# Two-part x1, later statistics, weight pieces on POOL and a lighter tail in a transformer layer

## The chip, the cores and the metric

One core of a Trainium2 chip. The core has five engines that run side by side, each with its own instruction stream served in order: PE (TensorE, matrix products), DVE (VectorE), ACT (ScalarE), POOL (GpSimd) and SP (SyncE, which here only issues transfers). They meet through semaphores. The metric is the device time of one execution in microseconds; lower is better.

## The reference

One post-norm transformer layer on 16 batch elements of 256 positions and 256 channels, in float32:

```
qkv = x @ Wqkv + bqkv                  # 16 query heads of 16, 4 key/value heads (shared)
prob = softmax(q k / 16);  a = (prob v) @ Wout + bout
x1 = layernorm(x + a)
gate, up = split(x1 @ tern(w_gate_up).T)        # 2 x 1024 channels
h = rms_norm(silu(gate) * up)
out = layernorm(x1 + h @ tern(w_proj).T)
```

`tern` makes a weight ternary: in bfloat16, by groups of 64, scale = mean(abs(w)), q = clip(round(w / scale), -1, 1), and w + (q * scale - w) with the rounding of each step.

## The kernel before

Float32 products are made of two passes: a tensor is split into a high part, rounded to a shorter format, and a low part, the rest, and both are multiplied with the same weights. x1 (transposed) and h are split this way.

The work is cut into slots. Batch element b has its steps at fixed offsets from slot 8b, so 8 slots after one element the next one does the same step, and up to six elements are in the pipeline at once. Every engine has a function `slot(n)` that goes through its own steps in a written order; a step runs if slot n minus its offset falls on an element (`once`) or on a chunk s = 0 to 7 of one (`chunk`). Slots 0 to 63 and 128 to the end are written out, slots 64 to 127 are a loop of 16-slot bodies. What an engine does in a slot, and in which order, is fixed by this code; semaphores only make it wait.

The steps of one element that matter here, with their offsets:

- Attention: raw scores for the row maxima from offset 9 (`max_scores` on PE, `take_maximum` on DVE, two per slot, called i = 0 and 1: "max0" and "max1"), exponentials from 15, products with v from 16.
- Offset 27: output projection on PE (PROJ_O); DVE adds the residual (O_ADD, L890), takes the statistics (`bn_stats` L893, `bn_aggr` L897); POOL makes the reciprocal root (RSTD1, L944 and L922).
- Offset 28: DVE scales r1 to x1 (LN1_APPLY, L881). Offset 29: PE transposes x1 (X1_T, L552) into a bank of `short_ps`, ACT copies the high part (X1_HIGH). Offset 30: DVE makes the low part (X1_LOW, L765).
- Offsets 31 to 38, one chunk per slot: gate and up products on PE (`gate_up`, L507), tanh on ACT, gated (L817) and h_f (L824) on DVE; one slot later ACT makes h_hi and the square, POOL h_lo (L928) and the running sum of squares (L933); two slots later `down` on PE (L521).
- Offset 40: sum of squares over partitions, mean, root. Offset 42: second residual and statistics on DVE, root on POOL (RSTD2). Offset 44: POOL scales to y_out (LN2_APPLY, L940), SP stores.

The three banks `short_ps` are shared by all short products by a table (BANK_TABLE); the transpose of x1 uses the bank that max0 of the same slot has used before it, and waits until that maximum is taken.

The order on POOL within a slot (L924): h_lo and sum of squares; LN2_APPLY; RSTD1; ADD_BOUT; Q_LOW; the weight piece; INV; RSTD2. On DVE (L811): max0; gated; h_f; X1_LOW; SHIFT_SPLIT[0]; LN2_STATS; max1; MEAN_SQ; PV_DIVIDE; V_COPY; LN1_APPLY; SHIFT_SPLIT[1]; weight piece; O_ADD with the statistics; K_LOW.

The ternary weights are made in 12 pieces in slots 1 to 27: ACT reads a piece in slot W_READ (L661), one slot later DVE makes sums, scale and three tensor operations on w_hat (`tern_weights`, L790) and POOL two more (L957 to L963); PE transposes the piece (`turn_weights`, L452) four slots after the read and ACT places it one slot after that. `keep_clock` (L560) adds small products on PE in slots 2 to 29.

Of the kernel before, what the change touches and what calls it, by code (L numbers as in the profile page):

```python
# [76 lines left out]
O_ADD = 27  # L77
RSTD1 = 27
X1_HIGH = 29
# [26 lines left out]
W_READ = (1, 2, 3, 5, 8, 10, 12, 14, 16, 18, 20, 22)  # L106
W_MAKE, W_TURN, W_PLACE = 1, 4, 5
W_LATER = 9
CLOCK_FROM, CLOCK_TO = 2, 30

LAST = SLOTS * B + STORE
LOOP_FROM, BODY = 64, 2 * SLOTS
LOOPS = (SLOTS * B - LOOP_FROM) // BODY
# [71 lines left out]


def previous_use(slot, position, uses):

    for back in range(slot.t + 1):
        earlier = Slot(slot.t - back, slot.it)
        for use in sorted(uses, key=lambda u: -u[1]):
            st = earlier.once(use[0])
            if st and (back or use[1] < position):
                return st, use
    return None


def postln_layer(nc, x, Wqkv, bqkv, Wout, bout, w_gate_up, w_proj, out):  # L200
    ctx = ExitStack()
    with ctx:
# [17 lines left out]
        w_sign = sb("w_sign", [P, 2, PG, Q_GROUP], BF16)  # L220
        w_hat = sb("w_hat", [P, 2, PG, Q_GROUP], BF16)
        w_sum = sb("w_sum", [P, PG])
        w_scale = sb("w_scale", [P, PG], BF16)
        w_half = sb("w_half", [P, PG], BF16)
# [132 lines left out]
        def piece(n, later):  # L357

            return W_READ.index(n.t - later) if n.it is None and n.t - later in W_READ else None

        block = ctx.enter_context(nc.Block())

# [79 lines left out]
        def _(pe):  # L442
# [9 lines left out]
            def turn_weights(c):  # L452

                pe.wait_ge(w_pool, 2 * (c + 1))
                if c >= 2:
                    pe.wait_ge(w_ev, c - 1)
                flat = w_hat[:, c % 2].rearrange("p g e -> p (g e)")
# [49 lines left out]
            def gate_up(n, st):  # L507
                wait(pe, x1T_lo, st.count(1, 1))
                if st.it is None and st.b == 0 and st.s == 0:
                    pe.wait_ge(w_ev, len(pieces))  # L510
                if alternate(n, st) and n.t - SLOTS < TWO_BANKS and st.s == 1:
                    wait(pe, exp_done, SLOTS * B)
                wait(pe, h_done, st.count(8, st.s - 1 if n.it is None and n.t > TWO_BANKS else st.s))
                for half in range(2):
                    c = half * F + st.s * P
                    last = products(gate_up_bank(n, st, half),
                                    [wguT[:, k, c:c + P] for k in range(DT) for _ in range(2)],
                                    [x1T[a][:, st.par, k, :] for k in range(DT) for a in range(2)])
                last.then_inc(ffn_made, 1)
# [40 lines left out]
            def keep_clock(n, count):  # L560

                if n.it is not None or not CLOCK_FROM <= n.t < CLOCK_TO:
                    return
                turned = sum(at + W_TURN < n.t for at in W_READ)
                if turned:
                    pe.wait_ge(w_ev, turned - 1)
                for _ in range(count):
                    pe.matmul(turn_banks[turned % 2][:, 0, 0:P], ident[:], ident[:], start=True, stop=True)

            def slot(n):  # L570
# [63 lines left out]
                if (c := piece(n, W_TURN)) is not None:  # L634
                    turn_weights(c)
# [17 lines left out]
        def _(act):  # L653
# [5 lines left out]
            def read_weights(c):  # L659

                raw = pieces[c][0]  # L661
                act.wait_ge(w_loaded[c], 16)
                if c >= 2:
                    act.wait_ge(w_pool, 2 * (c - 1))
# [12 lines left out]
            def slot(n):  # L677
# [71 lines left out]
                if (c := piece(n, W_PLACE)) is not None:  # L749
# [10 lines left out]
        def _(dve):  # L760
# [18 lines left out]
            def shift_rows(n, st, half):  # L779
# [8 lines left out]
                                         ).then_inc(shift_split, 1)  # L788

            def tern_weights(c):  # L790
# [4 lines left out]
                dve.tensor_scalar(w_scale[:], w_sum[:], 1.0 / Q_GROUP, 1e-8, ALU.mult, ALU.max).then_inc(w_red, 1)  # L795
                dve.wait_ge(w_red, 3 * c + 2)
                dve.tensor_scalar(w_half[:], w_scale[:], 0.5, None, ALU.mult).then_inc(w_red, 1)
                dve.wait_ge(w_red, 3 * c + 3)
                if c >= 2:
                    dve.wait_ge(w_tr, c - 1)  # L800
                half = w_half[:].unsqueeze(2).broadcast_to([P, PG, Q_GROUP])
                scale = w_scale[:].unsqueeze(2).broadcast_to([P, PG, Q_GROUP])

                hat = w_hat[:, c % 2]
                for i, (a, b, op) in enumerate(((w_abs[:, c % 2], half, ALU.is_gt), (hat, scale, ALU.mult),
                                                (hat, w_sign[:, c % 2], ALU.mult))):
                    if i:
                        dve.wait_ge(w_dve, 3 * c + i)
                    dve.tensor_tensor(hat, a, b, op).then_inc(w_dve, 1)  # L809

            def slot(n):  # L811
                if st := n.chunk(MAX0):
                    take_maximum(n, st, 0)
                if st := n.chunk(GATE0):

# [3 lines left out]
                if st := n.chunk(H0):  # L819
# [5 lines left out]
                                      ).then_inc(h_done, 1)  # L825
                if st := n.once(X1_LOW):
                    wait(dve, x1T_hi, st.count(1, 1))
                    low(x1T[1][:, st.par], both(n, "x1"), x1T[0][:, st.par]).then_inc(x1T_lo, 1)
                if st := n.once(SHIFT_SPLIT[0]):
                    shift_rows(n, st, 0)  # L830
                if st := n.once(LN2_STATS):

# [54 lines left out]
                if st := n.once(O_ADD):  # L887
                    wait(dve, o_made, st.count(1, 1))
                    wait(dve, bout_added, st.count(1, 1))
                    dve.tensor_tensor(r1[:], both(n, "o"), res[:, st.par], ALU.add).then_inc(r1_done, 1)  # L890
                    wait(dve, r1_done, st.count(1, 1))
                    for t in range(TT):
                        dve.bn_stats(st1[:, t, :], r1[:, t, :]).then_inc(bn1_done, 1)  # L893
                    wait(dve, bn1_done, st.count(TT, TT))
                    dve.sem_inc(waited, 1)
                    for t in range(TT):
                        dve.bn_aggr(mv1[:, t, :], st1[:, t, :]).then_inc(var1_done, 1)  # L897
                if st := n.once(K_LOW):
# [7 lines left out]
        def _(pool):  # L906
# [17 lines left out]
            def slot(n):  # L924
                if st := n.chunk(H_LOW0):
# [3 lines left out]
                                       h_p[0][:, st.s % 4, :].bitcast(F32), ALU.subtract).then_inc(h_lo, 1)  # L929
                    if st.s:  # L930
# [26 lines left out]
                if (c := piece(n, W_MAKE)) is not None:  # L957

                    pool.wait_ge(w_dve, 3 * (c + 1))
                    hat = w_hat[:, c % 2]  # L960
                    pool.tensor_tensor(hat, hat, w_bf[:, c % 2], ALU.subtract).then_inc(w_pool, 1)
                    pool.wait_ge(w_pool, 2 * c + 1)
                    pool.tensor_tensor(hat, hat, w_bf[:, c % 2], ALU.add).then_inc(w_pool, 1)  # L963
# [33 lines left out]
```

## Time and profile before

| | |
|---|---|
| median of 3 runs | 621.06 us (619.04 to 621.45) |
| profiled execution | 616.0 us |
| its span, first to last instruction | 614.1 us |
| mean granted TensorE clock | 0.971 of full speed |
| busy: PE, DVE, ACT, POOL | 554.9, 442.1, 369.9, 327.6 us |
| chain that ended last: PE, DVE, issue, POOL | 68%, 20%, 5%, 3% |

The profile shows one execution. Busy time is the time in which an engine works on an instruction; a product's end is modelled, so a busy PE isn't PE at its peak. The chain that ended last goes back from the last instruction, at each step to what released it or to the instruction before it on its engine. A granted clock of 1.0 is 2.4 GHz, 0.5 is 1.2 GHz.

### The profile page before, as it was taken

Reading aid. Unit: us, or ns where it says so; the run is one execution under the profiler, and the core shown is the slowest. Engines: PE = TensorE matmul, PEld = TensorE weight load, DVE = VectorE, ACT = ScalarE, POOL = GpSimd, SP = SyncE. Lnnn points to the kernel's source line nnn. Section 1 sums busy time; section 2 is a strip of 40 time slices with the busy share of each in tenths; the row PEclk is TensorE's granted clock in tenths of the full one; section 3 lists DMA queues with packets and bytes.
Section 4 is the critical chain, followed back from the end, with each engine's and each line's share of the span. In section 5 each row is a group of like instructions: output and inputs, shape, how many; then the busy total and the mean of one; then the engine's idle time right before and its main releaser. Section 6 shows DMA issues by size and latency. Waiting matters only on the chain.

```text
span 614.1 us, 14165 instructions
## 1 busy us (share of the span) xinstructions
PE 554.9 (90%) x4368; PEld 467.1 (76%) x4368; DVE 442.1 (72%) x1034; ACT 369.9 (60%) x738; POOL 327.6 (53%) x436
## 2 busy tenths in 40 slices
PE   5768979999999999999999999999999999999782
PEld 5657768778888887878787888788887877777772
DVE  7885875777777777786777777877777787855751
ACT  4453745576666666757566666666666756566441
POOL 5432331243645555555637473646555555566975
PEclk9687999999999999999999999999999999999996
DMA  6963454454352617062534435342617070101001
GB/s 226 159 139 45 84 83 89 79 97 70 77 107 59 124 45 139 4 148 37 136 47 103 78 77 103 78 104 63 119 44 138 23 141 4 36 2 36 18 1 35
DMA packets 53932, 49.08 MB, mean 80 GB/s; under 512 B 6144, under 2 KB 53888, under 8 KB 53888
## 3 DMA queue, kind: packets, MB, share of 16 engines
q1 hardware_dynamic: 51152, 47.60, 37.8%
q10 hardware_dynamic: 2736, 0.92, 0.7%
q8 instruction: 24, 0.39, 0.3%
q14 instruction: 20, 0.16, 0.1%
HBM read 33.29 MB, written 14.68 MB: 78 GB/s over the span
## 4 chain that ended last, share of the span: by engine, by line
PE 68%; DVE 20%; issue 5%; POOL 3%; ACT 1%; DMA 1%; ACTq 0%; POOLq 0%; DVEq 0%; SPq 0%
PE ffn_ps L447 17%; PE short_ps L447 11%; PE pv_ps L544 10%; PE short_ps L494 8%; PE down_ps L529 7%; PE exp_ps L503 7%; PE short_ps L552 5%; DVE w_hat L809 3%; DVE row_max L776 3%; DVE gated L817 2%; DVE st L893 2%; DVE r L890 2%; DVE x1T_lo L765 2%; DVE h_f L824 1%; DVE w_sum L793 1%
## 5 line engine op out<-in xcount | busy, mean ns | idle before, releaser
L776 DVE TENSOR_REDUCE row_max<-short_ps 128x2 f32<-128x512 f32 x256 | 173.7, 682 | 64.5 <-PE short_ps L494 64.4
L928 POOL TENSOR_TENSOR h_lo<-h_f,h_hi 128x256 fp32r<-128x256 f32 x128 | 94.6, 739 | 191.2 <-ACT h_hi L672 180.9
L690 ACT ACTIVATE probs<-exp_ps 128x1024 f32<-128x1024 f32 x128 | 130.9, 1023 | 37.3 <-PE exp_ps L503 34.0
L447 PE MATMUL ffn_ps<-x1T_hi,wguT 128*128 128x256 f32 x480 | 125.0, 293 | 15.9 <-DVE h_f L824 9.0
L494 PE MATMUL short_ps<-k_st,q_st 65*128 65x256 f32 x512 | 116.5, 309 | 13.0 <-DVE row_max L776 12.7
L447 PE MATMUL ffn_ps<-x1T_lo,wguT 128*128 128x256 f32 x480 | 119.3, 282 | 0.0
L681 ACT ACTIVATE tanh<-ffn_ps 128x256 f32<-128x256 f32 x120 | 45.8, 382 | 118.9 <-PE ffn_ps L447 101.9
L447 PEld LDWEIGHTS ffn_ps<-x1T_hi,wguT 128*128 128x128 f32 x480 | 90.8, 189 | 23.0 <-DVE h_f L824 11.1
L494 PEld LDWEIGHTS short_ps<-k_st,q_st 65*128 65x128 f32 x512 | 82.1, 192 | 23.6 <-DVE row_max L776 11.1
L447 PEld LDWEIGHTS ffn_ps<-x1T_lo,wguT 128*128 128x128 f32 x480 | 91.0, 189 | 0.0
L933 POOL TENSOR_TENSOR sq_sum<-sq_sum,h_sq 128x256 f32<-128x256 f32 x112 | 83.2, 743 | 0.0
L529 PE MATMUL down_ps<-wpT,h_hi 128*128 128x256 f32 x256 | 76.2, 320 | 5.9 <-POOL h_lo L928 5.9
L503 PE MATMUL exp_ps<-q_st,k_st 67*128 67x512 f32 x256 | 81.4, 399 | 0.2
L544 PE MATMUL pv_ps<-probs,v_ones 128*32 128x256 f32 x1024 | 68.5, 385 | 0.0
L529 PE MATMUL down_ps<-wpT,h_lo 128*128 128x256 f32 x256 | 66.8, 283 | 0.0
L529 PEld LDWEIGHTS down_ps<-wpT,h_hi 128*128 128x128 f32 x256 | 48.8, 191 | 19.5 <-issue 11.5
L817 DVE SCALAR_TENSOR_TENSOR gated<-tanh,ffn_ps 128x256 f32<-128x256 f32 x120 | 49.3, 410 | 18.9 <-ACT tanh L681 18.9
L824 DVE TENSOR_TENSOR h_f<-gated,ffn_ps 128x256 f32<-128x256 f32 x120 | 50.5, 421 | 5.4 <-DVE gated L817 1.6
L672 ACT ACTIVATE h_hi<-h_f 128x256 fp32r<-128x256 f32 x128 | 52.3, 409 | 1.2 <-DVE h_f L824 1.2
L529 PEld LDWEIGHTS down_ps<-wpT,h_lo 128*128 128x128 f32 x256 | 49.0, 191 | 0.4
L447 PE MATMUL short_ps<-xT,wqkv 128*128 128x256 f32 x192 | 48.2, 388 | 0.0
L722 ACT ACTIVATE h_sq<-h_f 128x256 f32<-128x256 f32 x112 | 45.7, 408 | 0.0
(98 smaller groups left out, 892.7 us busy)
## 6 DMA issues: line engine op xcount, KB each, us to landing
q_st<-q_dram SPq DMA_DIRECT2D x128, 128.0 KB, 4.1
q_dram<-q_p SPq DMA_DIRECT2D x16, 512.0 KB, 3.0
xn<-in_L_attn_x_dram SPq DMA_DIRECT2D x16, 256.0 KB, 4.5
k_st<-k_dram SPq DMA_DIRECT2D x64, 64.0 KB, 2.6
res<-in_L_attn_x_dram SPq DMA_DIRECT2D x16, 256.0 KB, 3.2
out_dram<-y_out SPq DMA_DIRECT2D x16, 256.0 KB, 2.2
wgu_raw<-in_L_ffn_w_gate_up_dram SPq DMA_DIRECT2D x8, 256.0 KB, 6.5
k_dram<-k_p SPq DMA_DIRECT2D x16, 128.0 KB, 3.1
```

The source lines that it names most:

```text
L447: last = pe.matmul(dst, a, b, start=start and i == 0, stop=stop and i == len(pairs) - 1)
L494: last = pe.matmul(bank[:, t * S:(t + 1) * S], q_st[0:PAD, st.par, head, t * P:(t + 1) * P], k_st[0:PAD, st.par, st.s % 4, :], start=True, ...
L503: last = pe.matmul(exp_ps[:, t, :], k_st[:, st.par, st.s % 4, t * P:(t + 1) * P], q_st[:, st.par, first_head(st.s):first_head(st.s) + 5:4, ...
L529: last = pe.matmul(down_ps[:, t, :], h_p[a][:, st.s % 4, t * P:(t + 1) * P], wpT[:, st.s, :], start=(st.s == 0 and t == 0 and a == 0), sto ...
L544: last = pe.matmul(pv_ps[r:r + 32, s % 4 // 2, :], v_ones[:, st.par, t, s % 4, :], probs[:, s % 4, t, i, :], start=(t == 0), stop=(t == TT ...
L672: return act.activation(dst, src, ACT.Identity)
L690: act.activation(probs[:, st.s % 4], exp_ps[:], ACT.Exp).then_inc(exp_done, 1)
L776: dve.tensor_reduce(row_max[:, st.par, head * TT:(head + 1) * TT], short(n, f"max{i}")[:].rearrange("p (t k) -> p t k", t=TT), AX.X, ALU.m ...
L817: dve.scalar_tensor_tensor(gated[:, st.s % 2, :], tanh[:, st.s % 2, :], 1.0, gate_up_bank(n, st, 1), ALU.add, ALU.mult).then_inc(gated_don ...
L824: dve.tensor_tensor(h_f[:, st.s % 2, :], gated[:, st.s % 2, :], gate_up_bank(n, st, 0), ALU.mult).then_inc(h_done, 1)
L928: pool.tensor_tensor(h_p[1][:, st.s % 4, :], h_f[:, st.s % 2, :], h_p[0][:, st.s % 4, :].bitcast(F32), ALU.subtract).then_inc(h_lo, 1)
L933: pool.tensor_tensor(sq_sum[:, st.par, :], sq_sum[:, st.par, :], h_sq[:, st.s % 2, :], ALU.add).then_inc(h_summed, 1)
```

## The change

Five edits, none of which changes what is computed:

1. `gate_up` waits for the high part of x1, makes its four products with it (two halves, two row blocks), then waits for the low part and makes the four with that.
2. The statistics of the first normalization are a step LN1_STATS of their own at offset 28, on DVE behind h_f; RSTD1 on POOL goes from 27 to 28. LN1_APPLY stays at 28.
3. From the fifth weight piece on, two of DVE's three tensor operations on w_hat are done by POOL; w_hat has four buffers instead of two, w_scale two. The transposes of pieces 1 to 3 come in slots 8, 9, 10 instead of 6, 7, 9.
4. From slot 136 on (`late`), the scaling to y_out is done by DVE instead of POOL, and X1_LOW stands ahead of gated.
5. For the last element, DVE adds the squares instead of POOL.

```diff
+LN1_STATS = 28
-RSTD1 = 27
+RSTD1 = 28
-W_MAKE, W_TURN, W_PLACE = 1, 4, 5
+W_MAKE = 1
+W_TURN = (5, 8, 9, 10, 12, 14, 16, 18, 20, 22, 24, 26)
+W_POOL_FROM = 4
+LATE = SLOTS * (B + 1)
+def late(n):
+    return n.it is None and n.t >= LATE
+def sums_on_dve(st):
+    return st.it is None and st.b == B - 1
...
 # PE, gate_up
-                wait(pe, x1T_lo, st.count(1, 1))
+                wait(pe, x1T_hi, st.count(1, 1))
...
-                for half in range(2):
-                    c = half * F + st.s * P
-                    last = products(gate_up_bank(n, st, half),
-                                    [wguT[:, k, c:c + P] for k in range(DT) for _ in range(2)],
-                                    [x1T[a][:, st.par, k, :] for k in range(DT) for a in range(2)])
+                for a in range(2):
+                    if a:
+                        wait(pe, x1T_lo, st.count(1, 1))
+                    for half in range(2):
+                        c = half * F + st.s * P
+                        first = a == 0 and (half == 0 or alternate(n, st))
+                        for k in range(DT):
+                            last = pe.matmul(gate_up_bank(n, st, half), wguT[:, k, c:c + P], x1T[a][:, st.par, k, :],
+                                             start=first and k == 0, stop=a == 1 and k == DT - 1,
+                                             skip_group_check=True)
...
 # DVE, slot
+                if (st := n.once(X1_LOW)) and late(n):
+                    x1_low(n, st)
                 if st := n.chunk(GATE0):
...
+                if st := n.once(LN1_STATS):
+                    wait(dve, r1_done, st.count(1, 1))
+                    for t in range(TT):
+                        dve.bn_stats(st1[:, t, :], r1[:, t, :]).then_inc(bn1_done, 1)
...
+                if (st := n.chunk(H_LOW0)) and st.s and sums_on_dve(st):
+                    wait(dve, h_squared, st.count(8, st.s + 1))
+                    wait(dve, h_summed, st.count(FT - 1, st.s - 1))
+                    dve.tensor_tensor(sq_sum[:, st.par, :], sq_sum[:, st.par, :], h_sq[:, st.s % 2, :], ALU.add
+                                      ).then_inc(h_summed, 1)
+                if (st := n.once(LN2_APPLY)) and late(n):
...
 # DVE, tern_weights
+                hat = w_hat[:, c % 4]
+                dve.tensor_tensor(hat, w_abs[:, c % 2], half, ALU.is_gt).then_inc(w_dve, 1)
+                if c < W_POOL_FROM:
...
 # POOL, slot
-                if st := n.once(LN2_APPLY):
+                if (st := n.once(LN2_APPLY)) and not late(n):
...
+                    if c >= W_POOL_FROM:
+                        pool.tensor_tensor(hat, hat, scale, ALU.mult).then_inc(w_pool, 1)
+                        pool.wait_ge(w_pool, w_pool_count(c) + 1)
+                        pool.tensor_tensor(hat, hat, w_sign[:, c % 2], ALU.mult).then_inc(w_pool, 1)
```

## Rows read from the trace of the kernel before

**Rows 1.** The page, part 1: busy time, share, instructions.
```profile
PE 554.9 (90%) x4368; PEld 467.1 (76%) x4368; DVE 442.1 (72%) x1034; ACT 369.9 (60%) x738; POOL 327.6 (53%) x436
```
**Rows 2.** Busy time by stretch: stretch, length, each engine, clock, DMA, GB/s.
```profile
300.00:400.00 100.00, 97.07 (x790) 81.22 (x791) 76.15 (x186) 65.39 (x133) 56.91 (x77) 1.00 0.42 85
```
**Rows 3.** The chain that ended last: start, us, what.
```profile
367.62 0.94 PE ffn_ps L447 x8
```
**Rows 4.** Waits from 120 to 510 us: total us, times, longest.
```profile
PE ffn_ps L447 <- DVE h_f L824: 6.3, 12, 0.6
...
PE ffn_ps L447 <- DVE x1T_lo L765: 5.5, 12, 0.5
```
**Rows 5.** Timeline, slots 27 to 29 of one element: start, us, instruction.
```profile
360.70 0.75 DVE L893 BATCH_NORM_STATS2 st<-r 128x6 f32<-128x256 f32 x2
...
361.61 0.25 DVE L897 BATCH_NORM_AGGREGATE mv<-st 128x2 f32<-128x6 f32 x2 [0.16 <-DVE st L893]
...
361.94 0.19 POOL L944 TENSOR_TENSOR ve<-mv,ln_eps 128x2 f32<-128x2 f32 x1 [1.45 <-DVE mv L897]
...
362.21 0.70 POOL L922 TENSOR_TENSOR rstd<-ve,minus_half 128x2 f32<-128x2 f32 x1
...
363.50 0.73 POOL L928 TENSOR_TENSOR h_lo<-h_f,h_hi 128x256 fp32r<-128x256 f32 x1 [0.59 <-ACT h_hi L672]
...
363.73 1.40 DVE L881 TENSOR_SCALAR x<-r,mv,rstd 128x256 f32<-128x256 f32 x2
...
364.19 0.79 POOL L933 TENSOR_TENSOR sq_sum<-sq_sum,h_sq 128x256 f32<-128x256 f32 x1
...
364.96 2.47 POOL L940 TENSOR_SCALAR y_out<-r,mv,rstd 128x256 f32<-128x256 f32 x2
...
365.05 0.68 DVE L776 TENSOR_REDUCE row_max<-short_ps 128x2 f32<-128x512 f32 x1
...
366.48 0.66 PE L552 MATMUL short_ps<-ident,x 128*128 128x128 f32 x4
```
**Rows 6.** Timeline, the same scaling for the first element.
```profile
104.72 0.73 DVE L881 TENSOR_SCALAR x<-r,mv,rstd 128x256 f32<-128x256 f32 x2
```
**Rows 7.** Busy time by stretch, around idle times of PE; the clock is third from last.
```profile
592.70:595.00 2.30, 0.03 (x1) 0.00 (x0) 1.43 (x6) 1.11 (x3) 1.61 (x4) 1.00 0.00 0
595.85:599.20 3.35, 3.35 (x19) 3.35 (x18) 0.84 (x2) 0.99 (x3) 3.35 (x4) 0.51 0.02 5
55.10:57.20 2.10, 0.01 (x1) 0.01 (x1) 1.93 (x4) 1.37 (x3) 1.17 (x2) 1.00 0.00 0
...
39.70:41.70 2.00, 0.02 (x1) 0.05 (x2) 1.97 (x5) 0.00 (x0) 1.21 (x2) 1.00 0.72 153
43.00:53.10 10.10, 7.43 (x35) 6.88 (x34) 6.05 (x14) 3.77 (x6) 2.30 (x2) 0.50 0.87 111
```
**Rows 8.** The chain that ended last, weight piece 5 of 12 pieces.
```profile
39.18 0.70 DVE w_hat L809
...
39.91 0.43 DVE w_hat L809
```
**Rows 9.** Waits of PE from 30 to 89 us.
```profile
PE short_ps L494 <- DVE row_max L776: 11.3, 7, 2.7
PE short_ps L557 <- DVE row_max L776: 2.1, 1, 2.1
```
**Rows 10.** Timeline, PE behind weight pieces 4 and 10.
```profile
32.43 0.51 PE L494 MATMUL short_ps<-k_st,q_st 65*128 65x256 f32 x2 [0.84 <-DVE row_max L776]
...
79.04 0.51 PE L494 MATMUL short_ps<-k_st,q_st 65*128 65x256 f32 x2 [1.39 <-DVE row_max L776]
```
**Rows 11.** The costliest groups: busy us, mean ns, idle before and its releaser.
```profile
L961 POOL TENSOR_TENSOR w_hat<-w_hat,w_bf 128x512 bf16<-128x512 bf16 x12 | 13.9, 1161 | 45.5 <-DVE w_hat L809 45.5
```
**Rows 12.** Timeline, the last 20 us.
```profile
595.03 0.38 PE L529 MATMUL down_ps<-wpT,h_hi 128*128 128x256 f32 x1 [2.29 <-POOL h_lo L928]
...
609.07 2.43 POOL L940 TENSOR_SCALAR y_out<-r,mv,rstd 128x256 f32<-128x256 f32 x2 [0.24 <-POOL rstd L922]
```

More of the change, by code:

```diff
@@ L220, in postln_layer @@
         w_sign = sb("w_sign", [P, 2, PG, Q_GROUP], BF16)
-        w_hat = sb("w_hat", [P, 2, PG, Q_GROUP], BF16)
+        w_hat = sb("w_hat", [P, 4, PG, Q_GROUP], BF16)
         w_sum = sb("w_sum", [P, PG])
-        w_scale = sb("w_scale", [P, PG], BF16)
+        w_scale = sb("w_scale", [P, 2, PG], BF16)
         w_half = sb("w_half", [P, PG], BF16)
@@ L359, in piece, with turned_piece, w_dve_count, w_pool_count @@
             return W_READ.index(n.t - later) if n.it is None and n.t - later in W_READ else None
+        def turned_piece(n, later):
+            return W_TURN.index(n.t - later) if n.it is None and n.t - later in W_TURN else None
+        def w_dve_count(c):
+            return 3 * min(c, W_POOL_FROM) + max(c - W_POOL_FROM, 0)
+        def w_pool_count(c):
+            return 2 * min(c, W_POOL_FROM) + 4 * max(c - W_POOL_FROM, 0)
         block = ctx.enter_context(nc.Block())
@@ L452, in turn_weights @@
             def turn_weights(c):
-                pe.wait_ge(w_pool, 2 * (c + 1))
+                pe.wait_ge(w_pool, w_pool_count(c + 1))
                 if c >= 2:
                     pe.wait_ge(w_ev, c - 1)
-                flat = w_hat[:, c % 2].rearrange("p g e -> p (g e)")
+                flat = w_hat[:, c % 4].rearrange("p g e -> p (g e)")
                 for i, at in enumerate(pieces[c][2]):
@@ L563, in keep_clock @@
                     return
-                turned = sum(at + W_TURN < n.t for at in W_READ)
+                turned = sum(at < n.t for at in W_TURN)
                 if turned:
@@ L633, in slot @@
                     turn(bank, [att[:, t, m * P:(m + 1) * P] for m in range(DT) for t in range(TT)], att_turned)
-                if (c := piece(n, W_TURN)) is not None:
+                if (c := turned_piece(n, 0)) is not None:
                     turn_weights(c)
@@ L663, in read_weights @@
                 if c >= 2:
-                    act.wait_ge(w_pool, 2 * (c - 1))
+                    act.wait_ge(w_pool, w_pool_count(c - 1))
                 flat = w_bf[:, c % 2].rearrange("p g e -> p (g e)")
@@ L748, in slot @@
                                 .bitcast(F32), shift_p[half][part][:].bitcast(F32)).then_inc(shift_loaded[half], 16)
-                if (c := piece(n, W_PLACE)) is not None:
+                if (c := turned_piece(n, 1)) is not None:
                     act.wait_ge(w_tr, c + 1)
@@ L788, in shift_rows, with x1_low @@
                                          ).then_inc(shift_split, 1)
+            def x1_low(n, st):
+                wait(dve, x1T_hi, st.count(1, 1))
+                low(x1T[1][:, st.par], both(n, "x1"), x1T[0][:, st.par]).then_inc(x1T_lo, 1)
             def tern_weights(c):
@@ L794, in tern_weights @@
                 dve.wait_ge(w_red, 3 * c + 1)
-                dve.tensor_scalar(w_scale[:], w_sum[:], 1.0 / Q_GROUP, 1e-8, ALU.mult, ALU.max).then_inc(w_red, 1)
+                dve.tensor_scalar(w_scale[:, c % 2], w_sum[:], 1.0 / Q_GROUP, 1e-8, ALU.mult, ALU.max).then_inc(w_red, 1)
                 dve.wait_ge(w_red, 3 * c + 2)
-                dve.tensor_scalar(w_half[:], w_scale[:], 0.5, None, ALU.mult).then_inc(w_red, 1)
+                dve.tensor_scalar(w_half[:], w_scale[:, c % 2], 0.5, None, ALU.mult).then_inc(w_red, 1)
                 dve.wait_ge(w_red, 3 * c + 3)
-                if c >= 2:
-                    dve.wait_ge(w_tr, c - 1)
+                if c >= 4:
+                    dve.wait_ge(w_tr, c - 3)
                 half = w_half[:].unsqueeze(2).broadcast_to([P, PG, Q_GROUP])
[L802 to L809, printed above, removed]
+                scale = w_scale[:, c % 2].unsqueeze(2).broadcast_to([P, PG, Q_GROUP])
+                hat = w_hat[:, c % 4]
+                dve.tensor_tensor(hat, w_abs[:, c % 2], half, ALU.is_gt).then_inc(w_dve, 1)
+                if c < W_POOL_FROM:
+                    dve.wait_ge(w_dve, 3 * c + 1)
+                    dve.tensor_tensor(hat, hat, scale, ALU.mult).then_inc(w_dve, 1)
+                    dve.wait_ge(w_dve, 3 * c + 2)
+                    dve.tensor_tensor(hat, hat, w_sign[:, c % 2], ALU.mult).then_inc(w_dve, 1)
             def slot(n):
@@ L825, in slot @@
                                       ).then_inc(h_done, 1)
-                if st := n.once(X1_LOW):
-                    wait(dve, x1T_hi, st.count(1, 1))
-                    low(x1T[1][:, st.par], both(n, "x1"), x1T[0][:, st.par]).then_inc(x1T_lo, 1)
+                if st := n.once(LN1_STATS):
+                    wait(dve, r1_done, st.count(1, 1))
+                    for t in range(TT):
+                        dve.bn_stats(st1[:, t, :], r1[:, t, :]).then_inc(bn1_done, 1)
+                    wait(dve, bn1_done, st.count(TT, TT))
+                    dve.sem_inc(waited, 1)
+                    for t in range(TT):
+                        dve.bn_aggr(mv1[:, t, :], st1[:, t, :]).then_inc(var1_done, 1)
+                if (st := n.once(X1_LOW)) and not late(n):
+                    x1_low(n, st)
                 if st := n.once(SHIFT_SPLIT[0]):
                     shift_rows(n, st, 0)
+                if (st := n.chunk(H_LOW0)) and st.s and sums_on_dve(st):
[4 more added lines that the diff above has]
+                if (st := n.once(LN2_APPLY)) and late(n):
+                    wait(dve, rstd2_done, st.count(1, 1))
+                    wait(dve, stored[st.par], st.count2(16, 0))
+                    for t in range(TT):
+                        dve.tensor_scalar(y_out[:, st.par, t, :], r2[:, t, :], mv2[:, t, 0:1], rstd2[:, t:t + 1],
+                                          ALU.subtract, ALU.mult).then_inc(y_done, 1)
                 if st := n.once(LN2_STATS):
@@ L890, in slot @@
                     dve.tensor_tensor(r1[:], both(n, "o"), res[:, st.par], ALU.add).then_inc(r1_done, 1)
[L891 to L897, printed above, removed]
                 if st := n.once(K_LOW):
@@ L929, in slot @@
                                        h_p[0][:, st.s % 4, :].bitcast(F32), ALU.subtract).then_inc(h_lo, 1)
-                    if st.s:
+                    if st.s and not sums_on_dve(st):
                         wait(pool, h_squared, st.count(8, st.s + 1))
@@ L957, in slot @@
                 if (c := piece(n, W_MAKE)) is not None:
-                    pool.wait_ge(w_dve, 3 * (c + 1))
-                    hat = w_hat[:, c % 2]
+                    pool.wait_ge(w_dve, w_dve_count(c + 1))
+                    hat = w_hat[:, c % 4]
+                    if c >= W_POOL_FROM:
+                        scale = w_scale[:, c % 2].unsqueeze(2).broadcast_to([P, PG, Q_GROUP])
+                        pool.tensor_tensor(hat, hat, scale, ALU.mult).then_inc(w_pool, 1)
+                        pool.wait_ge(w_pool, w_pool_count(c) + 1)
+                        pool.tensor_tensor(hat, hat, w_sign[:, c % 2], ALU.mult).then_inc(w_pool, 1)
+                        pool.wait_ge(w_pool, w_pool_count(c) + 2)
                     pool.tensor_tensor(hat, hat, w_bf[:, c % 2], ALU.subtract).then_inc(w_pool, 1)
-                    pool.wait_ge(w_pool, 2 * c + 1)
+                    pool.wait_ge(w_pool, w_pool_count(c + 1) - 1)
                     pool.tensor_tensor(hat, hat, w_bf[:, c % 2], ALU.add).then_inc(w_pool, 1)
```

## The prediction, made before the changed kernel was run

> **What bounds the kernel now.** First the page's busy shares: PE is busy 90% of the span, the first thing to suspect [rows 1]. Then the busy time by stretch, because a share is a mean over stages: between 300 and 400 us PE is busy 97.07 of 100 us, while DVE has 24 and POOL 43 us free [rows 2]. There a microsecond saved on DVE or POOL is worth nothing unless PE waits for it, and a wait given to PE is paid in full. The chain that ended last runs there over PE; the eight products of a slot take 0.94 us of it [rows 3]. Last the waits between 120 and 510 us: those of PE for DVE are 5.5 us for the low part of x1 and 6.3 us for h_f, twelve times each, 0.46 and 0.52 us per element, and twelve elements in 390 us make some 32.5 us for one [rows 4].
>
> **High part of x1 first.** The eight products stay eight; only the four with the high part may start before the low part is there. Four take half of 0.94, 0.47 us, about the wait of 0.46 us [rows 3, 4], so the wait goes. I count it 13 times (elements 1 to 13) and 0.6 us for element 14; behind element 0 PE waits for a transfer anyway, and element 15 is in the tail's sum. 13 x 0.47 + 0.6 = 6.7 us gained; bounds 0 and 7.4 us, for eight products held by something else and for all sixteen elements.
>
> **Statistics later.** On DVE the statistics go from slot 27 of an element to 28 (0.75 + 0.16 + 0.25 = 1.16 us, L893 and L897 [rows 5]), on POOL the reciprocal root that needs them too. The use, LN1_APPLY on DVE, stays in slot 28, and the transpose of x1 on PE in 29. But slot 28 is also slot 44 of the element two before, and on POOL y_out stands ahead of RSTD1 in program order. I follow elements 2 to 13 in the trace's own times [rows 5]:
> - DVE takes max0, gated and h_f first, then the statistics: they end at 364.1 to 364.3, not 361.86.
> - POOL does h_lo at 363.50, then sq_sum, and reaches y_out at 364.96, for 2.47 us, to 367.43. Only then come ve1 (0.27 us from its start to the root's) and the root, 0.70 us: 368.4, where it was 362.9.
> - DVE stands at LN1_APPLY. The scaling ran at 363.73 and the next maximum at 365.05; now 368.45 and, 1.32 us on, 369.77. Queued behind the waiting instruction are the next slot's max0, gated and h_f, all 4.7 us late.
> - PE turns x1 in slot 29 into the bank which that max0 frees (0.67 us, to 370.44): at 370.5 instead of 366.48. So 4.0 us in which PE, served in order, has nothing to do.
> Alone, without POOL's h_lo beside it, the scaling takes 0.73 us instead of 1.32 [rows 6], which makes 3.4 us the lower bound; DVE's whole 4.7 us is the upper. Elements 0 and 1 have no y_out before them and for 14 it is on DVE: 0, 1.2 us (the root behind sq_sum, at 366.0, scaling ahead of max0 as above) and 1.5 us. Sum: 12 x 4.0 + 2.7 = 50.7 us lost, 43 to 60.
>
> **TensorE's clock.** It follows the stall. PE did nothing for 2.3 us up to 595.0, and from 595.85 to 599.2 the granted clock was 0.51, the level of 1.2 GHz; after an idle time of 2.0 us up to 41.7 it was 0.50 for ten microseconds (43 to 53.1); after 2.1 us up to 57.2 it stayed at full [rows 7]. Two microseconds thus lost the clock two times in three; 4 us I take to lose it nearly always. The stretch of 3.35 us costs 3.35 x (1 - 0.51) = 1.6 us, the ten microseconds would cost 5. I take 1.6, because behind this stall PE is busy throughout, as in the tail, and not with gaps as at 43: 12 x 1.6 = 19 us lost. Bounds 0 and 60.
> The Trainium skill (TensorE: Matmul & The Clock Gate, section "HAM oscillation — how this bites in real kernels") tells of a kernel whose wait in every pass puts the clock back to half in every pass. By that rule the loss comes all twelve times, by the row of 55.1 to 57.2 it may stay away in some.
>
> **Weight pieces.** For pieces 4 to 11 two of DVE's three tensor operations go to POOL: 0.70 and 0.43 us on the chain, with the steps between them 1.14 us a piece [rows 8]; all eight are on that chain. The saving ends where PE no longer waits. Between 30 and 89 us PE waited 11.3 + 2.1 us for maxima [rows 9]: behind piece 4 only 0.84 us and behind pieces 9 and 10 together 1.39 us [rows 10], behind the other five over 1.14. So 0.84 + 5 x 1.14 + 1.39 = 7.9 us gained. POOL now has four operations of 1.16 us per piece instead of two, and idled 45.5 us before twelve pieces [rows 11], 3.8 a piece, which hides the 2.3 more; if not, q_lo of elements 1 and 2 would be late, by 1.3 us, for rows that PE reads 10 us later. Turning pieces 1 to 3 later lets PE reach slot 9 up to 0.9 us sooner, but then it stands for an eviction in slot 11: nothing. Bounds 5 and 11 us (the upper if the slow ten microseconds go as well).
>
> **Tail.** The last scaling takes 2.43 us on POOL [rows 12] and 0.73 on DVE [rows 6]: 1.7 us, beside nothing. Before it POOL works without a break from 594.25 to 603.58 (five h_lo, five sums, y_out of element 14), and PE waits for it, once 2.29 us [rows 12]. Sums (3.6 us) and y_out (2.4) go; then the ring of product, tanh, gated, h_f, h_hi, h_lo, down binds, with 0.4 to 0.7 us more for DVE in each slot. Of the 6.0 us I count 2.7 as won, by following that ring over the last five slots. Together 4.4 us (1.7 to 7.7), element 15's own statistics included.
> The Trainium skill (SBUF — State Buffer, section "SBUF: two separate sides") says that a DVE operation with two SBUF inputs and a GpSimd one shut each other out for the whole instruction. Each of the seven sums moved to DVE would then wait for an h_lo or hold it up, and of the 2.7 us little would be left.
>
> **Sum.** - 6.7 + 50.7 + 19 - 7.9 - 4.4 = + 50.7 us against the profiled execution's 616.0 us (614.1 of span, 1.9 around it). The median of the runs, 621.06, lies 5.1 us above; the sum is added to it: 671.8, so 672 us.
>
> **Rivals.**
> - The clock holds: the same stall without the 19 us, 653 us. For it the row of 55.1 to 57.2 [rows 7]; against it that this idle time is twice as long.
> - The clock stays low as long as at 43: 5 us for 1.6, 12 x 3.4 = 41 us more, 713 us.
> - Half the stall, 2 us per element and the clock held: 24 + 2.7 - 6.7 - 7.9 - 4.4 = + 8 us, 629 us. It needs work that PE could take up meanwhile; it has 3 us free in 100 [rows 2].
> - The other side, no stall. One point decides: whether DVE has the root when it comes to the scaling, at 364.8. For that the root must be issued before y_out (364.96) and before sq_sum too. Then only - 6.7 - 7.9 - 4.4 = - 19 us remain, 602 us; with sq_sum alone before the root each element loses 1.2 us, 14 + 2.7 in all, and it is 619 us. For it speaks only that POOL is free for a while before h_lo; against it that the statistics end after h_lo has begun, and that POOL's rows keep the code's order [rows 5].
>
> **How the numbers follow.** Stall and lost clock 0.58, stall and held clock 0.22, long lost clock 0.05, half a stall 0.07, root before y_out 0.08 (half of it at 602, half at 619). The likeliest gives 672 us, with 655 to 690 as its own range. 645 to 692 takes in the second case and leaves out the last three. A measurement tells 0.5% (3 us) from no change, so: faster 0.06, same 0.03, slower 0.91.
>
> **What would show it.** On POOL ve1 and the root behind y_out in slot 28. On DVE some 3.5 us of idle time before the scaling of x1, released by POOL. On PE 4 us before the transpose of x1, 37 to 39 us from element to element in place of 32.5, a granted clock near 0.5 behind it, and no wait for x1T_lo. In the first 90 us, PE's waits for maxima near 5.5 us instead of 13.4. At the end no y_out on POOL. It is wrong if the root comes before y_out, or if an element stays under 34.5 us.

## The result, and the profile after

The changed kernel took 669.22 us (median of 4 runs, 667.28 to 674.44), the kernel before 620.05 us beside it: ratio 1.081, 95% interval 1.074 to 1.088. The forecast was 672 us. The profiled execution took 667.28 us with a span of 665.5. Medians and ratios below leave out runs more than 1.5% above the fastest of the same kernel: one run of 613.20 us, of the kernel with edit 3 undone.

First the page of the changed kernel, to be laid beside [rows 1]: busy time by engine, the granted clock in 40 slices, the chain by engine, and one group of part 5.

```profile
PE 571.0 (86%) x4368; PEld 485.2 (73%) x4368; DVE 442.0 (66%) x1033; ACT 370.3 (56%) x738; POOL 330.4 (50%) x437
...
PEclk9689999999798989999898989989898989989996
...
PE 52%; POOL 17%; issue 15%; DVE 8%; DMA 4%; ACT 2%; SPq 2%; POOLq 0%; ACTq 0%; DVEq 0%
...
L581 PE MATMUL short_ps<-ident,x 128*128 128x128 f32 x64 | 14.2, 361 | 53.8 <-DVE row_max L805 49.2
```

PE's share fell from 90% to 86%, and the clock line shows an 8 at every second or third slice of 16.6 us, about once per element. The one group to look for is the last line: the transposes of x1 are 14.2 us of work, with 53.8 us of idle time of PE ahead of them, 49.2 of it released by a maximum on DVE.

The waits from 120 to 560 us (us in total, times, longest), elements 2 to 13, beside [rows 4]:

```profile
PE short_ps L581 <- DVE row_max L805: 45.1, 12, 4.1
DVE x L935 <- POOL rstd L969: 40.6, 12, 3.6
```

The wait for x1T_lo is gone, as meant, and two new ones are there twelve times each: 3.4 us on DVE for the root, 3.8 us on PE for the maximum behind it. The timeline of one element, slots 28 and 29 (start, length, instruction), beside [rows 5]:

```profile
388.57 0.74 POOL L975 TENSOR_TENSOR h_lo<-h_f,h_hi 128x256 fp32r<-128x256 f32 x1 [3.01 <-ACT h_hi L701]
389.00 0.25 DVE L869 BATCH_NORM_AGGREGATE mv<-st 128x2 f32<-128x6 f32 x2 [0.16 <-DVE st L865]
389.16 0.67 DVE L805 TENSOR_REDUCE row_max<-short_ps 128x2 f32<-128x512 f32 x1
389.27 0.74 POOL L980 TENSOR_TENSOR sq_sum<-sq_sum,h_sq 128x256 f32<-128x256 f32 x1
390.00 2.44 POOL L987 TENSOR_SCALAR y_out<-r,mv,rstd 128x256 f32<-128x256 f32 x2
392.40 0.20 POOL L991 TENSOR_TENSOR ve<-mv,ln_eps 128x2 f32<-128x2 f32 x1
392.67 0.71 POOL L969 TENSOR_TENSOR rstd<-ve,minus_half 128x2 f32<-128x2 f32 x1
393.35 0.72 POOL L975 TENSOR_TENSOR h_lo<-h_f,h_hi 128x256 fp32r<-128x256 f32 x1
393.42 1.53 DVE L935 TENSOR_SCALAR x<-r,mv,rstd 128x256 f32<-128x256 f32 x2 [3.60 <-POOL rstd L969]
394.88 0.68 DVE L805 TENSOR_REDUCE row_max<-short_ps 128x2 f32<-128x512 f32 x1
395.61 1.11 PE L581 MATMUL short_ps<-ident,x 128*128 128x128 f32 x4 [4.03 <-DVE row_max L805]
```

Read it downwards. The statistics end at 389.25. POOL is then in h_lo, goes on to sq_sum and to the 2.44 us of y_out, and only at 392.67 to the root. DVE stands 3.60 us at the scaling; the maximum queued behind it comes at 394.88, and PE, which may not overwrite that bank before, stands 4.03 us. The same stretch by windows (start and end, length, busy time of PE, PEld, DVE, ACT, POOL, then granted clock, DMA share, GB/s), beside [rows 7]:

```profile
392.00:395.60 3.60, 0.00 (x0) 0.00 (x0) 2.18 (x4) 0.00 (x0) 2.73 (x5) 0.96 0.48 145
395.60:398.90 3.30, 3.29 (x16) 3.29 (x17) 1.77 (x5) 0.60 (x1) 0.00 (x0) 0.52 0.03 6
398.90:402.00 3.10, 3.10 (x24) 2.78 (x23) 2.59 (x6) 2.02 (x4) 0.75 (x2) 1.00 0.19 53
```

PE does nothing in the first, works without a gap at 0.52 of the clock (the level of 1.2 GHz) in the second, and at full clock in the third. In quarter-microsecond windows over the whole trace each of the twelve stalls has such a stretch at its end (from 207.5, 245.25, 282.75, ... 545.5, 583.0), 3.25 to 3.5 us long but for the first, 6.75 us from 166.75. They are some 37.6 us apart, which is the time of one element now.

### The profile page after: what moved, and what is told of

Its sections match the earlier page's. It is cut to its first block, busy times and chain, and to the rows that moved or that the text cites. A ratio compares the mean times of both kernels' runs of the same rounds, so it can differ in the third digit from the quotient of the medians.

```text
span 665.5 us, 14163 instructions
## 1 busy us (share of the span) xinstructions
PE 571.0 (86%) x4368; PEld 485.2 (73%) x4368; DVE 442.0 (66%) x1033; ACT 370.3 (56%) x738; POOL 330.4 (50%) x437
## 4 chain that ended last, share of the span: by engine, by line
PE 52%; POOL 17%; issue 15%; DVE 8%; DMA 4%; ACT 2%; SPq 2%; POOLq 0%; ACTq 0%; DVEq 0%
PE ffn_ps L545 13%; PE down_ps L558 7%; PE short_ps L470 6%; PE short_ps L517 6%; PE exp_ps L526 6%; PE short_ps L581 6%; PE pv_ps L573 5%; POOL y_out L987 4%; POOL h_lo L975 4%; POOL sq_sum L980 3%; DVE row_max L805 2%; DVE x L935 2%; POOL res L999 1%; POOL q_p L1003 1%; DMA xn<-in_L_attn_x_dram 1%
## 5 line engine op out<-in xcount | busy, mean ns | idle before, releaser
L545 PE MATMUL ffn_ps<-x1T_hi,wguT 128*128 128x256 f32 x480 | 86.4, 305 | 8.3 <-DVE h_f L860 8.2
L558 PE MATMUL down_ps<-wpT,h_hi 128*128 128x256 f32 x256 | 80.1, 333 | 4.3 <-POOL h_lo L975 4.3
L545 PE MATMUL ffn_ps<-x1T_lo,wguT 128*128 128x256 f32 x480 | 81.1, 293 | 0.0
L545 PEld LDWEIGHTS ffn_ps<-x1T_hi,wguT 128*128 128x128 f32 x480 | 70.1, 203 | 12.6 <-issue 7.5
L980 POOL TENSOR_TENSOR sq_sum<-sq_sum,h_sq 128x256 f32<-128x256 f32 x105 | 77.8, 741 | 0.0
L558 PE MATMUL down_ps<-wpT,h_lo 128*128 128x256 f32 x256 | 70.4, 295 | 0.0
L545 PEld LDWEIGHTS ffn_ps<-x1T_lo,wguT 128*128 128x128 f32 x480 | 69.4, 200 | 0.5
L581 PE MATMUL short_ps<-ident,x 128*128 128x128 f32 x64 | 14.2, 361 | 53.8 <-DVE row_max L805 49.2
L853 DVE SCALAR_TENSOR_TENSOR gated<-tanh,ffn_ps 128x256 f32<-128x256 f32 x120 | 49.2, 410 | 15.5 <-ACT tanh L710 15.5
L581 PEld LDWEIGHTS short_ps<-ident,x 128*128 128x128 f32 x64 | 8.9, 176 | 61.1 <-DVE row_max L805 55.8
L935 DVE TENSOR_SCALAR x<-r,mv,rstd 128x256 f32<-128x256 f32 x32 | 22.5, 744 | 46.2 <-POOL rstd L969 46.2
```

What stands on the lines that cost most here:

```text
L545: last = pe.matmul(gate_up_bank(n, st, half), wguT[:, k, c:c + P], x1T[a][:, st.par, k, :], start=first and k == 0, stop=a == 1 and k == D ...
L558: last = pe.matmul(down_ps[:, t, :], h_p[a][:, st.s % 4, t * P:(t + 1) * P], wpT[:, st.s, :], start=(st.s == 0 and t == 0 and a == 0), sto ...
L581: last = pe.transpose(bank[:, i * P:(i + 1) * P], blk, ident[:])
```

## The experiments

Each kernel ran beside the kernel before on the same chip, in three sets (the first three kernels below; the fill of 30 and the three with an edit undone; the fill of 16, the root in between and the last two); ratios are to that. "Undone" refers to the numbers of the five edits.

**Which order on POOL costs the time.** Root of LN1 ahead of y_out, nothing else altered:

```diff
 # POOL, slot, behind h_lo and sq_sum
+                if st := n.once(RSTD1):
+                    ...
                 if (st := n.once(LN2_APPLY)) and not late(n):
                     ...
-                if st := n.once(RSTD1):
-                    ...
```

> The changed kernel with one edit: on POOL the reciprocal root of the first normalization (RSTD1) stands ahead of y_out (LN2_APPLY) in the slot, nothing else. My theory (the root stood behind y_out's 2.44 us): the root is then only behind h_lo and sq_sum, DVE's idle time before the scaling of x1 falls from 3.6 to about 1.1 us, PE's before the transpose from 4.0 to about 1.2 us, and the clock holds; 669 - 12 x 2.8 - 19 = about 616 us. Rival (the loss is that the statistics stand in the scaling's own slot at all, wherever the root stands): the loss stays mostly, over 645 us.

Measured: 616.98 us, ratio 0.995 (0.991 to 0.999). One instruction pair of 2.44 us, passed by a root of 0.71, is worth 52 us, the clock's loss included (no stretch of half clock is left between 52 and 601 us); the expectation gave 12 x 2.8 + 19 = 53 for it. The rest of the wait is still there, over the whole run:

```profile
DVE x L935 <- POOL rstd L969: 16.9, 16, 1.2
```

Edit 2 undone, statistics and root back in slot 27:

```diff
-LN1_STATS = 28
-RSTD1 = 28
+RSTD1 = 27
```

> The changed kernel with the second edit undone: statistics in slot 27 behind the residual, RSTD1 in 27; the other four edits stay. My theory: the whole stall and the clock's loss go, and the other edits are worth 19 us against the kernel before: 601 us, 0.97 of it. Rival (the stall comes from products in the new order or from POOL's weight work, and the statistics only show it): it stays above 640 us. Second rival (the other edits are worth nothing): 620 us.

Measured: 600.64 us, ratio 0.967 (0.958 to 0.976). The other four edits together are a gain of some 20 us, and edit 2 is the whole of the loss.

Edit 2 alone on the kernel before, the converse:

> The kernel before with the second edit alone: statistics and RSTD1 at 28. My theory: 12 x 4.0 us and more for element 14 (its y_out is still on POOL, so 4 us instead of 1.5), 19 us of clock, and no gain: 620 + 53 + 19 = 692 us, and PE's wait for x1T_lo partly hidden by the slow products, so 685 to 692. Rival (the stall needs the other edits too): under 640 us.

Measured: 699.89 us, ratio 1.130 (1.119 to 1.141). The sign and the mechanism agree, the size misses the expectation by 8 us at the least. Two windows, the two waits and two transposes of x1 of this kernel, of elements 7 and 15:

```profile
366.50:374.00 7.50, 5.02 (x23) 4.79 (x24) 4.83 (x10) 1.11 (x3) 1.68 (x3) 0.54 0.24 72
407.50:412.00 4.50, 4.43 (x23) 4.30 (x24) 2.35 (x7) 1.04 (x3) 0.00 (x0) 0.62 0.03 8
```

```profile
DVE x L890 <- POOL rstd L924: 52.1, 16, 4.0
PE short_ps L553 <- DVE row_max L777: 49.0, 13, 4.0
```

```profile
368.98 1.12 PE L553 MATMUL short_ps<-ident,x 128*128 128x128 f32 x4 [4.00 <-DVE row_max L777]
...
658.98 1.09 PE L553 MATMUL short_ps<-ident,x 128*128 128x128 f32 x4 [5.41 <-DVE x L890]
```

PE's waits for the maximum are those of the changed kernel, 49.0 us against 49.2. What the expectation left out is element 15: its root too stands behind a y_out that is still on POOL here, and PE stood 5.41 us ahead of its transpose, against 3.09 in the changed kernel. Between the evictions of x1's high part, from element 14 to 15, pass 26.2 us in this kernel and 21.0 in the kernel before: 5.3 us more. From 13 to 14 it is 34.0 against 28.2, 5.8 us for the stall of 4 and its clock.

The clock has a smaller part in it. Of the fourteen low stretches at the stalls of this kernel (elements 2 to 15), seven are 6.75 to 7 us long and the others 3.25 to 3.5. In the long ones the clock fell while PE still stood: at 366.75, when the stall lasted to 368.98, so the gap in the first window (5.02 of 7.50 us busy) is the end of the stall itself. Behind it PE worked 4.5 us at the low clock without a gap, and 3.7 us behind a short one (407.57 to 411.25); 0.8 us more at half clock is an estimated 0.4 us for a long stretch. From element 1 to 13 the kernel with edit 2 alone loses 66.9 us against the kernel before, the changed kernel 64.9 against the one with edit 2 undone. Why the clock fell sooner in some stalls stays open.

**Root in between.** Root behind h_lo but ahead of sq_sum and y_out:

```diff
 # POOL, slot, between h_lo and sq_sum
+                if sr := n.once(RSTD1):
+                    ...
                 if (st := n.chunk(H_LOW0)):
                     # sq_sum
```

> The changed kernel with the root on POOL between h_lo and the sum of squares, so also ahead of y_out. My theory (what is left of the stall with the root only ahead of y_out, 1.1 us of DVE's wait per element, is POOL's sq_sum of 0.75 us before it): DVE's wait for the root falls to 0.3 to 0.4 us per element and the time by 12 x 0.7 = 8 us, to 609 us; the sum of squares has time. Rival (the statistics end so late that the root waits for them and not for POOL): 615 to 617 us.

Measured: 610.02 us, ratio 0.985 (0.981 to 0.989). The waits from 120 to 510 us, of the kernel with the root behind sq_sum and then of this one:

```profile
DVE x L935 <- POOL rstd L969: 13.8, 12, 1.2
PE short_ps L581 <- DVE row_max L805: 12.1, 12, 1.0
```

```profile
PE short_ps L581 <- DVE row_max L805: 6.6, 12, 0.6
DVE x L935 <- POOL rstd L969: 6.1, 12, 0.5
```

DVE waits 0.5 us in place of 1.15 and PE 0.55 in place of 1.0: 5.5 us of the 7 gained. So the wait has three parts: y_out (2.44 us), sq_sum (0.7 us), and what remains of slot 28 itself. In time, the clock's loss included, they are 52 us (669.2 to 617.0), 7 us (617.0 to 610.0) and 10 us (610.0 to 600.2, where the statistics are back in slot 27). The last part is seen on DVE in this kernel: the statistics end at 359.74, ve and the root take POOL until 360.79, and only then can the scaling run.

```profile
359.49 0.25 DVE L869 BATCH_NORM_AGGREGATE mv<-st 128x2 f32<-128x6 f32 x2 [0.16 <-DVE st L865]
...
360.09 0.70 POOL L969 TENSOR_TENSOR rstd<-ve,minus_half 128x2 f32<-128x2 f32 x1
...
360.83 1.14 DVE L935 TENSOR_SCALAR x<-r,mv,rstd 128x256 f32<-128x256 f32 x2 [0.51 <-POOL rstd L969]
```

**What the clock costs.** Products that nobody reads, on PE ahead of the transpose of x1, in elements 2 to 13, so that PE is busy while it would stand. Their number was 30 in the first kernel and 16 in the second:

```diff
                 if st := n.once(X1_T):
+                    if st.it is not None or 2 <= st.b <= 13:
+                        for _ in range(30):        # then 16
+                            pe.matmul(short_ps[0][64:128, 2 * P:3 * P], ident[:, 64:128], ident[:],
+                                      start=True, stop=True, tile_position=(0, 64))
```

> The changed kernel with 30 products of 64 by 128 columns (identity by identity, into free partitions and columns of a bank, result unused) on PE ahead of the transpose of x1, for elements 2 to 13. They take some 3.4 us at full clock and fit into the 4.0 us in which PE waits. My theory (the lost clock costs 1.6 us per element, apart from the stall): the granted clock stays near 1.0 and the time falls by 15 to 19 us, to 650 to 654 us. Rival (the slow products lie beside other waits and cost nothing, the whole loss is the stall): within 3 us of 669 us, or above by what the fill does not fit into.

Measured: 684.08 us, ratio 1.105 (1.100 to 1.111), far from both. Its timeline shows why:

```profile
398.39 6.76 PE L644 MATMUL short_ps<-ident 128*64 128x128 f32 x60
...
401.75 0.68 DVE L809 TENSOR_REDUCE row_max<-short_ps 128x2 f32<-128x512 f32 x1
...
405.08 0.66 PE L581 MATMUL short_ps<-ident,x 128*128 128x128 f32 x4
```

30 products of this type run as 60 instructions and take 6.76 us; the maximum was done at 402.43, and the transpose waited 2.7 us more for the fill itself. The clock held (1.00 from 395 to 405 us). Less twelve times this overrun the time would be 652 us, within the theory's range; the rival, with the overrun added, would be at 701. With 16:

> As the kernel with 30 fill products, but 16 of them. The 30 ran as 60 instructions and took 6.76 us, 2.7 us longer than PE's wait; 16 take 3.6 us and fit. My theory (the clock's loss costs 1.5 us per element beside the stall): clock near 0.98 over the span, and 669 - 12 x 1.5 = 651 us. Rival (the slow products cost nothing): 669 us.

Measured: 653.01 us, ratio 1.055 (1.051 to 1.059).

```profile
387.54 0.66 PE L581 MATMUL short_ps<-ident,x 128*128 128x128 f32 x4 [0.40 <-DVE row_max L809]
```

```profile
380.00:400.00 20.00, 19.45 (x166) 16.86 (x167) 13.85 (x36) 10.48 (x23) 10.10 (x14) 1.00 0.58 105
```

```profile
DVE x L939 <- POOL rstd L973: 46.2, 16, 3.6
```

This one is clean: the transpose is still released by the maximum, DVE waits for the root as long as in the changed kernel (46.2 us in 16 waits there too), and the clock is 1.00 throughout. Doing more work, the kernel is 16 us faster than the changed one: 1.35 us per element is what the clock cost. From the eviction of x1's high part in element 1 to that in element 14 it takes 465.0 us, the changed kernel 482.0: 17.0 us, or 1.4 per element. What the stall alone costs is 653.0 - 600.2 = 53 us (600.2 is the mean of the two medians of the version with edit 2 undone), over elements 1 to 15.

**The four edits that stay.** Undone on top of the version with edit 2 undone: edit 3 and edit 1 by themselves, 4 and 5 together. Of edit 3 only the work on POOL is undone; the four buffers and the later transposes stay, and no run tests those. Edit 3:

```diff
-W_POOL_FROM = 4
+W_POOL_FROM = 12
```

> The changed kernel with the statistics back in slot 27 and, besides, all three tensor operations of every weight piece on DVE again (four buffers and the later transposes stay). My theory: the moved operations are worth 7.9 us, PE's waits for maxima in the first 90 us go back to about 13 us: 601 + 8 = 609 us, 0.980 of the kernel before. Rival (DVE's time there was hidden, the gain comes from elsewhere): 601 us, 0.967.

Measured: 608.45 us, ratio 0.980 (0.974 to 0.985). Edit 1:

```diff
 # PE, gate_up
-                wait(pe, x1T_hi, st.count(1, 1))
+                wait(pe, x1T_lo, st.count(1, 1))
```

> The changed kernel with the statistics back in slot 27 and the wait for the low part of x1 ahead of all eight products, whose new order stays. My theory: the wait is 0.46 us of each element and all of it is paid: 601 + 7 = 608 us, 0.979 of the kernel before, and the trace shows PE waiting for x1T_lo some 6 to 7 us. Rival (PE then waits as long for something else, such as h_f, so the early start bought nothing): 601 us.

Measured: 607.03 us, ratio 0.978 (0.974 to 0.981). Edits 4 and 5, `late` and `sums_on_dve` both made to return False:

> The changed kernel with the statistics back in slot 27 and, besides, the last scalings and the last element's sums on POOL again and X1_LOW behind h_f. My theory: the tail's edits are worth 4.4 us, 1.7 of it the last scaling: 601 + 4.4 = 605 us, 0.974. Rival (DVE and POOL hold each other up so that only the last scaling counts): 602.5 us, 0.970.

Measured: 604.51 us, ratio 0.974 (0.971 to 0.978). The times alone lie near each other's intervals; the eviction of x1's high part serves as a milestone for where each loses. In order: edit 2 undone (elements 0, 13 and 15), edit 3 undone too (element 0), edit 1 undone too (0 and 13), edits 4 and 5 undone too (15).

```profile
103.41 0.60 ACT L700 ACTIVATE x1T_hi<-short_ps 128x512 fp32r<-128x512 f32 x1 [2.13 <-PE short_ps L580]
...
520.06 0.60 ACT L700 ACTIVATE x1T_hi<-short_ps 128x512 fp32r<-128x512 f32 x1 [0.31 <-PE short_ps L580]
...
569.24 0.60 ACT L700 ACTIVATE x1T_hi<-short_ps 128x512 fp32r<-128x512 f32 x1 [2.33 <-PE short_ps L580]
```

```profile
109.53 0.60 ACT L700 ACTIVATE x1T_hi<-short_ps 128x512 fp32r<-128x512 f32 x1 [2.13 <-PE short_ps L580]
```

```profile
103.95 0.60 ACT L700 ACTIVATE x1T_hi<-short_ps 128x512 fp32r<-128x512 f32 x1 [2.12 <-PE short_ps L580]
...
526.82 0.60 ACT L700 ACTIVATE x1T_hi<-short_ps 128x512 fp32r<-128x512 f32 x1 [0.30 <-PE short_ps L580]
```

```profile
570.64 0.60 ACT L700 ACTIVATE x1T_hi<-short_ps 128x512 fp32r<-128x512 f32 x1 [1.39 <-PE short_ps L580]
```

With the weight work back on DVE, element 0 is 6.1 us later, and everything after it. Each trace is one execution, and this milestone moves from one to the next: in the ten profiled kernels with the weight work on POOL it lies between 101.1 and 105.7 us (mean 102.6), in the three with it on DVE at 107.5, 109.3 and 109.5. The two groups don't overlap, so the gain is shown, with some 6 us as its size. With the wait for the low part back, element 0 is on time (0.5 us), and from element 0 to 13 pass 422.9 us instead of 416.7: 6.2 us, or 0.48 per element. This stretch is steady: 416.5 to 416.7 us in all four profiled kernels that have the early start, the statistics in slot 27 and the weight work on POOL, and 418.6 in the one with that work on DVE. With the tail back on POOL, 34.3 us lie between element 15's eviction and the end of the span (604.9) instead of 30.5 (599.7), 3.8 us; but the last step up to that eviction, from element 14 to 15, is 0.8 us shorter there. From element 13 to the end it is 2.9 us, and 4.5 against the second run of the version with edit 2 undone. One expectation failed in its means: PE's waits for maxima in the first 89 us were to go back to 13 us when edit 3 was undone, and came to 7.6:

```profile
PE short_ps L516 <- DVE row_max L804: 7.6, 5, 3.2
```

The sum of these waits is thus no measure of what the edit saves; the milestone and the time are.

**Where the tail's gain comes from.** Edit 5 alone undone (the sums back on POOL, the scaling left on DVE), beside a second run of the version with edit 2 undone:

```diff
 def sums_on_dve(st):
-    return st.it is None and st.b == B - 1
+    return False
```

> The changed kernel with the statistics back in slot 27 and the last element's sums of squares on POOL again, the last scalings on DVE. My theory (POOL's queue binds in the last eight slots): of the 4.4 us of the tail, 1.7 are the last scaling and 2.7 come from POOL's two other loads, sums and y_out of element 14, in about equal parts: 602 us, 0.9695 of the kernel before. Rival (the sums' lock with h_lo eats their gain): 600.6 us, 0.967, as with the sums on DVE.

> The changed kernel with only the statistics back in slot 27, once more, beside the others of this call: 600.6 us, 0.967 of the kernel before, as the first time; it is the version that beats both kernels.

Measured: 601.99 us, ratio 0.973 (0.969 to 0.976), and 599.84 us, ratio 0.970 (0.966 to 0.973). The intervals overlap, and the spans of the profiled executions are 596.0 and 595.7 us: whether the sums on DVE gain anything stays open, and so does which half of the expectation holds. The version with edit 2 undone is repeated within 1 us, 600.64 and 599.84, and is faster than both kernels.

## Why the prediction was right

**The stall.** The steps are those of the forecast. From the start of h_lo on POOL to the end of the root it put 4.9 us (363.50 to 368.4); the rows show 4.8 (388.57 to 393.38), with sq_sum and y_out between. Its 12 x 4.0 + 2.7 = 50.7 us stand against 53 us in the fill of 16; a single stall is 3.76 us by the waits (45.1 / 12), between the bounds of 3.4 and 4.7. The order on POOL was the point that decides: moving the root ahead of y_out brings back 52 us, the clock's 16 among them.

**The clock.** It was lost twelve times in twelve, as by the Trainium skill (TensorE: Matmul & The Clock Gate, section "HAM oscillation — how this bites in real kernels"), and not two times in three as behind the idle times of 2 us in [rows 7]. That count left one out: PE also stood 2.06 us up to 88.09 in the kernel before, and the clock stayed at full, so it was two times in four. The price was 1.35 to 1.4 us each instead of 1.6: 16 to 17 us for 19. The rows of the low stretches (3.3 us at 0.52) give the 1.6; no run shows where the other 2 to 3 us went.

**High part first.** 6.8 us by the times (607.0 - 600.2), 6.2 by the milestones up to element 13, forecast 6.7. **Weight pieces.** 8.2 us by the times (608.4 - 600.2), some 6 by element 0, forecast 7.9; the size is about right, the account by single waits of PE was not borne out. **Tail.** 4.3 us by the times, 2.9 to 4.5 by the milestones, forecast 4.4. Of its parts the sums are unproven, so most of it is likely the two scalings; that is argued, not shown.

**The rivals.** "The clock holds" at 653 us is what the fill of 16 made true by force, at 653.0; the changed kernel itself is not there. The other side was priced at 619 us with sq_sum ahead of the root, and 617.0 was measured. With the root ahead of sq_sum too it was priced at 602 us, without a stall; built, this came to 610.0. That price was wrong by 8 us: such an order leaves a wait of 0.5 us per element on DVE and 0.55 on PE, because the statistics, ve and the root still stand between h_f and the scaling in slot 28. The 600.6 us belong to another kernel, with the statistics in slot 27. The long lost clock (713 us) did not come here: one stretch of twelve was 6.75 us and none 10.

**Luck in the number.** The measured terms add up to - 6.8 + 53 + 16 - 8.2 - 4.3 = + 50 us; the medians differ by 49.2, and the forecast was + 50.7. It is this close because the stall came out 2 us dearer and the clock 3 us cheaper than forecast, and the two cancel.

**Signs named beforehand.** All were seen but one in size: PE's waits for maxima in the first 89 us are 6.5 us (the two lines for row_max below), not 5.5.

```profile
PE short_ps L517 <- DVE row_max L805: 6.0, 5, 2.9
PE ffn_ps L597 <- ACT wguT L701: 0.9, 1, 0.9
PE short_ps L586 <- DVE row_max L805: 0.5, 1, 0.5
```

The 0.9 us for the eviction of wguT is the one in slot 11 to which the forecast gave the gain of the later transposes.

## What to carry to other kernels

A step moved by one slot is placed among everything that its engine already has in that slot: here that cost 53 us over the elements and 16 more through PE's clock, while four useful edits beside it were worth 20. Of these 69 us, 52 come from a root of 0.7 us that stood behind a scaling of 2.4 us, 7 from the sum of squares ahead of it, and 10 from the later slot itself. So write down the order in each in-order queue before and after a move, and ask who stands behind the instruction that now waits. Measure a disputed clock loss by filling the gap, with products short enough to end before the gap does.

## What the runs showed of the hardware

- At every idle time of PE of 4 us behind element 1 the granted clock went to near 0.5: twelve of twelve in the changed kernel, thirteen of thirteen in the kernel with edit 2 alone. The low stretch was 3.25 to 3.5 us long, or 6.75 to 7 us where the clock fell 1.1 us or more before PE worked again (one of the twelve, six of the thirteen). An idle time of 3.1 us up to 635.61 in the changed kernel left the clock at full, while one of 2.2 us up to 649.97 had half clock from 651.25 behind it:

```profile
632.51:635.61 3.10, 0.01 (x2) 0.04 (x1) 2.51 (x7) 0.99 (x3) 2.72 (x5) 1.00 0.25 85
637.00:640.00 3.00, 2.82 (x24) 2.62 (x23) 1.88 (x5) 1.89 (x6) 1.54 (x3) 1.00 0.00 0
651.25:654.75 3.50, 3.50 (x19) 3.50 (x18) 1.61 (x4) 1.34 (x5) 0.73 (x1) 0.51 0.22 75
```

- A product of the identity with itself, in f32 and 64 columns by 128, ran as two instructions of 0.11 us each: 60 in 6.76 us for 30 written, 32 in 3.71 us for 16.
- The same scaling on DVE took 0.73 us alone [rows 6], 1.53 us when it began together with an h_lo on POOL (above). DVE's sums in the tail of the changed kernel were held up in the same company:

```profile
648.85 0.42 DVE L877 TENSOR_TENSOR sq_sum<-sq_sum,h_sq 128x256 f32<-128x256 f32 x1
...
652.61 0.73 POOL L975 TENSOR_TENSOR h_lo<-h_f,h_hi 128x256 fp32r<-128x256 f32 x1 [2.01 <-ACT h_hi L701]
653.06 0.57 DVE L877 TENSOR_TENSOR sq_sum<-sq_sum,h_sq 128x256 f32<-128x256 f32 x1
...
655.17 0.73 POOL L975 TENSOR_TENSOR h_lo<-h_f,h_hi 128x256 fp32r<-128x256 f32 x1 [1.83 <-ACT h_hi L701]
655.62 0.57 DVE L877 TENSOR_TENSOR sq_sum<-sq_sum,h_sq 128x256 f32<-128x256 f32 x1
```

  With no h_lo beside it a sum takes 0.42 us. Begun while h_lo runs, it ends 0.28 or 0.29 us behind the end of h_lo in all six cases (653.63 against 653.34, 656.19 against 655.90), whatever time it had beside it. That agrees with the Trainium skill (SBUF — State Buffer, section "SBUF: two separate sides"), by which the two shut each other out. Here it cost 0.12 to 0.16 us a sum in five cases, where the sum started late in h_lo, and 0.33 in the sixth. Whether the scaling is slowed in the same way no row shows.
